# Ten of 24 state products of a scan chunk on VectorE instead of eight, and the engines' orders laid out anew

## The reference

```
delta = softplus(w_dt @ dts + b_dt)                # per batch, direction k, channel d, position t
h[t] = exp(delta[t] * A[d,n]) * h[t-1] + delta[t] * u[t] * B[n,t]
y[t] = sum over n of h[t] * C[n,t]  +  D * u[t]    # 16 states n, 192 channels d, 4096 positions t
```

## Time and profile before

| | us |
|---|---|
| median of 3 runs | 11698.7 (11697.71 to 11724.16) |
| the profiled execution | 11687.62 |
| its span | 11685.8 |
| VectorE busy | 10036.1 (86%) |
| GpSimd busy | 8772.1 (75%) |
| ScalarE busy | 8437.5 (72%) |
| TensorE busy | 9207.4 (79%) |

### The profile page before, as it was taken

One profiled execution on the slowest core, in us unless ns is written; L12 is line 12 of the kernel. 1 busy time (PEld: TensorE's weight loads), 2 busy tenths in 40 slices (PEclk: granted clock), 3 DMA queues, 4 the chain that ended last, 5 costly groups with the idle time before them and its releaser, 6 DMA issues. The chain is left out here.

```text
span 11685.8 us, 144402 instructions
## 1 busy us (share of the span) xinstructions
PE 9207.4 (79%) x34584; PEld 3443.5 (29%) x34584; DVE 10036.1 (86%) x6335; ACT 8437.5 (72%) x13829; POOL 8772.1 (75%) x4468
## 2 busy tenths in 40 slices
PE   8877777777777777777777777777777777588888
PEld 2322222222222222222222222222222222233333
DVE  7759999999899989999999899999999999866565
ACT  6767777777777777777777777777777777455555
POOL 0019999899899989999999899999999999521210
PEclk9988888888888888888888888888888888799999
DMA  3347777787777777777777777777777777643441
GB/s 103 122 127 185 183 187 184 178 187 186 183 180 185 187 183 181 186 187 183 184 185 188 179 183 185 185 182 181 185 186 184 187 186 182 149 112 94 100 108 49
DMA packets 577596, 1948.45 MB, mean 167 GB/s; under 512 B 106614, under 2 KB 111638, under 8 KB 562198
## 3 DMA queue, kind: packets, MB, share of 16 engines
q1 hardware_dynamic: 573714, 1938.65, 69.8%
q10 hardware_dynamic: 3076, 0.97, 0.1%
HBM read 1532.38 MB, written 406.85 MB: 166 GB/s over the span
## 5 line engine op out<-in xcount | busy, mean ns | idle before, releaser
L1108 POOL TENSOR_TENSOR dBu<-rep,shared 128x1024 f32<-128x1024 f32 x2304 | 4552.5, 1998 | 886.2 <-DMA rep<-dd_dram 833.5
L1116 POOL TENSOR_TENSOR h<-h,shared 128x1024 f32<-128x1024 f32 x2048 | 4020.7, 1972 | 728.6 <-DVE h L1068 728.0
L893 ACT ACTIVATE pd<-rep,a_now 128x1024 f32<-128x1024 f32 x2304 | 2556.1, 1109 | 362.7 <-DVE h L1068 200.9
L821 PE MATMUL py<-h,fold 128*32 128x512 f32 x8192 | 2447.8, 701 | 214.9 <-ACT y L968 214.9
L1068 DVE TENSOR_TENSOR_SCAN h<-pd,carry,dBu 128x1024 f32<-128x1024 f32 x960 | 2242.4, 2344 | 409.7 <-ACT pd L893 280.0
L1068 DVE TENSOR_TENSOR_SCAN pd<-pd,carry,dBu 128x1024 f32<-128x1024 f32 x768 | 1795.8, 2338 | 0.1
L821 PE MATMUL py<-shared,fold 128*32 128x512 f32 x3072 | 1479.6, 880 | 221.8 <-ACT y L968 173.3
L934 ACT ACTIVATE shared<-shared,turned_b 128x192 f32<-128x192 f32 x4096 | 1553.2, 442 | 15.5 <-ACT shared L921 5.4
L799 PE MATMUL pd<-eye,shared 128*128 128x128 f32 x6144 | 1006.9, 316 | 619.3 <-DVE h L1068 466.9
L1068 DVE TENSOR_TENSOR_SCAN h<-h,carry,pd 128x1024 f32<-128x1024 f32 x576 | 1308.8, 2326 | 43.2 <-PE pd L799 32.3
L799 PEld LDWEIGHTS pd<-eye,shared 128*128 128x128 f32 x6144 | 792.8, 159 | 1083.4 <-DVE h L1068 478.0
(11 more groups left out here) (174 smaller groups left out, 14120.2 us busy)
## 6 DMA issues: line engine op xcount, KB each, us to landing
rep<-dd_dram SPq DMA_DIRECT2D x1024, 768.0 KB, 13.0
shared<-bc_dram SPq DMA_DIRECT2D x3584, 128.0 KB, 4.6
u<-u_dram SPq DMA_DIRECT2D x128, 768.0 KB, 6.8
dd_dram<-LG SPq DMA_DIRECT2D x256, 384.0 KB, 4.0
dd_dram<-RL SPq DMA_DIRECT2D x256, 384.0 KB, 5.1
y_dram<-y SPq DMA_DIRECT2D x256, 384.0 KB, 8.1
shared<-y_dram SPq DMA_DIRECT2D x63, 1536.0 KB, 15.7
u_dram<-shared SPq DMA_DIRECT2D x32, 1536.0 KB, 7.5
```

Source lines behind the costliest of these rows:

```text
L821: last = mm(py[32 * g:32 * g + 32, t2(t)], fold[:, :], weighted(3 * j + g, k)[:, t2(t)], start=(j % 4 == 0), stop=(j % 4 == 3), skip_group ...
L893: go(dst, rep[:, half, 0, g, :], ACT.Exp, scale=a_now[:, column(i)]).then_inc(S.exped, 1)
L1108: nc.gpsimd.tensor_tensor(dBu[:, ring(c, p), :], rep[:, half, 1, g, :], BB[:, r, :], ALU.mult).then_inc(S.dbu, 1)
L1116: nc.gpsimd.tensor_tensor(turned(weighted(i, k), k), turned(kept(i, k), k), turned(CC[:, r, :], k), ALU.mult).then_inc(S.hc_pool, 1)
```

## The change

- `DVE_TILES` gains tiles 7 and 16. VectorE multiplies ten tiles of a chunk by C (eight so far), GpSimd fourteen (sixteen so far). `PLACES` goes from 8 to 7 and the product slots `PRODUCTS` from 4 to 5.
- TensorE's order: the first fold comes behind `add_up` of the next chunk's first half; `skip` comes behind the third fold; the fifth fold comes behind `add_up` of the second half.
- ScalarE's order: the copy of y's second half moves from step 2 to step 4, of the first half from 14 to 17; both copies of x_dbl and B now in step 23; `STEPS`, `SCALE` and `SCALE_NEXT` are shifted by a step or two.
- GpSimd's order: the two products fall out, and drives and products are interleaved anew.

```diff
--- before.py
+++ after.py
@@ -383,7 +383,7 @@
         psum = lambda name, shape: ctx.enter_context(nc.psum_tensor(name, shape, F32))
         S = a.sems
         BK = B * K
-        PLACES, PRODUCTS = 8, 4
+        PLACES, PRODUCTS = 7, 5
 
         a_neg, a_now = sb("a_neg", [128, K, NS]), sb("a_now", [128, NS])
         fold, eye128 = sb("fold", [128, 32]), sb("eye128", [128, 128])
@@ -408,7 +408,7 @@
         turned_b = sb("turned_b", [128, 2, TB, J])
         dBu = sb("dBu", [128, 4, T])
         h = sb("h", [128, PLACES, T + 4])
-        hC_last = sb("hC", [128, T])
+        hC_own = sb("hC", [128, PRODUCTS - 3, T])
         carry = sb("carry", [128, NS])
         y = sb("y", [HALF, T])
         pd = psum("pd", [128, 2, T])
@@ -427,7 +427,7 @@
 
         TRIPLES = ((0, 0), (0, 1), (0, 2), (0, 3), (1, 3), (1, 0), (1, 1), (1, 2))
         DRIVEN, TURNED, SCALED = 18, 6, 4 * TB
-        DVE_TILES = (0, 3, 4, 6, 15, 18, 19, 21)
+        DVE_TILES = (0, 3, 4, 6, 7, 15, 16, 18, 19, 21)
 
         def where(i):
             half, r = TRIPLES[i // 3]
@@ -459,7 +459,7 @@
             if is_kept(i):
                 return h[:, KEPT.index(i) % PLACES, 2:T + 2] if k < 2 else h[:, KEPT.index(i) % PLACES, 3:T + 3]
             slot = DVE_TILES.index(i) % PRODUCTS
-            return hC[:, slot, :] if slot < 3 else hC_last[:, :]
+            return hC[:, slot, :] if slot < 3 else hC_own[:, slot - 3, :]
 
         def state(i, k):
 
@@ -836,9 +836,9 @@
 
             def body(bk, k, c, left):
                 n, s = bk * NC + c, c % 2
-                reduce_states(n, k, 0)
                 if left:
                     add_up(n + 1, 0)
+                reduce_states(n, k, 0)
                 turn_back(bk, c, 9)
                 turn_back(bk, c, 10)
                 reduce_states(n, k, 1)
@@ -850,12 +850,12 @@
                 if left:
                     make_step(n + 1, 1)
                 turn_back(bk, c, 14)
+                reduce_states(n, k, 2)
                 skip(n, s, 0)
-                reduce_states(n, k, 2)
                 reduce_states(n, k, 3)
-                reduce_states(n, k, 4)
                 if left:
                     add_up(n + 1, 1)
+                reduce_states(n, k, 4)
                 skip(n, s, 1)
                 if left:
                     turn_du(n + 1, 1)
@@ -985,17 +985,16 @@
 
             STEPS = {1: [(absolute, 0)],
                      2: [(exp_abs, 0), (relu, 0), (one_plus, 0)],
-                     4: [(log, 0)],
-                     8: [(copy_delta, 0)],
+                     5: [(log, 0)],
+                     10: [(copy_delta, 0)],
                      11: [(copy_du, 0)],
-                     12: [(absolute, 1), (exp_abs, 1)],
-                     13: [(relu, 1)],
-                     14: [(one_plus, 1)],
-                     16: [(log, 1)],
+                     13: [(absolute, 1)],
+                     14: [(exp_abs, 1), (relu, 1), (one_plus, 1)],
+                     15: [(log, 1)],
                      18: [(copy_delta, 1)],
                      20: [(copy_du, 1)]}
-            SCALE = {0: 3, 2: 2, 3: 3, 4: 2, 5: 6, 6: 2, 7: 1}
-            SCALE_NEXT = {20: 5, 21: 3, 22: 2, 23: 3}
+            SCALE = {0: 3, 1: 2, 3: 2, 4: 4, 5: 2, 6: 6}
+            SCALE_NEXT = {20: 3, 21: 2, 22: 4, 23: 4}
 
             def run(bk, k, c, left, first, span):
                 n, s = bk * NC + c, c % 2
@@ -1010,14 +1009,14 @@
                         if c == NC - 1 and i + 2 == NS:
                             pick_a(bk + 1, (k + 1) % K)
                         expo(*((bk, k, c + 1) if c < NC - 1 else (bk + 1, (k + 1) % K, 0)), i + 2 - NS)
-                    if i == 2 and not first:
+                    if i == 4 and not first:
                         copy_y(n - 1, 1)
-                    if i == 14:
+                    if i == 17:
                         copy_y(n, 0)
                     if left:
                         for step, half in STEPS.get(i, ()):
                             step(n + 1, half)
-                        if left >= 2 and i == 22:
+                        if left >= 2 and i == 23:
                             copy_x_dbl(n + 2)
                         if left >= 2 and i == 23:
                             copy_b(n + 2, s)
@@ -1122,19 +1121,18 @@
             def body(bk, k, c, left):
                 n = bk * NC + c
                 drive(n, c, 3)
+                weigh(n, k, 1)
                 drive(n, c, 4)
-                weigh(n, k, 1)
+                drive(n, c, 5)
                 weigh(n, k, 2)
-                drive(n, c, 5)
                 drive(n, c, 6)
                 drive(n, c, 7)
                 drive(n, c, 8)
                 weigh(n, k, 5)
                 drive(n, c, 9)
                 drive(n, c, 10)
-                weigh(n, k, 7)
+                weigh(n, k, 8)
                 drive(n, c, 11)
-                weigh(n, k, 8)
                 weigh(n, k, 9)
                 weigh(n, k, 10)
                 weigh(n, k, 11)
@@ -1143,18 +1141,17 @@
                 weigh(n, k, 14)
                 drive(n, c, 12)
                 drive(n, c, 13)
-                weigh(n, k, 16)
+                drive(n, c, 14)
                 weigh(n, k, 17)
-                drive(n, c, 14)
                 drive(n, c, 15)
                 drive(n, c, 16)
                 drive(n, c, 17)
                 weigh(n, k, 20)
                 if left:
                     drive(n, c, 18)
-                    drive(n, c, 19)
                 weigh(n, k, 22)
                 if left:
+                    drive(n, c, 19)
                     drive(n, c, 20)
                 weigh(n, k, 23)
             chunk_loop(pool, body)
```

## The result

| | before | after |
|---|---|---|
| median of 4 runs each, us | 11702.44 | 11594.29 (11592.5 to 11613.69) |
| profiled execution, its span | 11687.62, 11685.8 | 11613.69, 11611.7 |
| scan phase, us a chunk | 72.49 | 71.75 |

The ratio is 0.9908 with a 95% interval of 0.9891 to 0.9925: 108 us faster, where 216 were forecast. The time lies within the range, the gain is half of what I had worked out. (The execution profiled after stands 20 us above its median.)

What follows compares the result with a forecast made beforehand. VectorE was taken to bound the kernel. Work 69.00 plus holes of 0.85, 0.3 and 0.65 gave 70.8 us a chunk against 72.49, 216 us less: 11472 profiled, 11482 in the median's terms; range 11370 to 11650.

Steps and rivals of the forecast that it cites:

- The work: VectorE's busy time a chunk: 66.35 us plus 2.65 for the two added products, 69.00 in all.
- The small rest: Small VectorE holes that remain: 0.65 us a chunk, a quarter of the 2.6 left of today's idling.
- the 70.6: VectorE's work a chunk, in us, by the rule that the next operation waits for an empty pipe; the sum didn't use it.
- ScalarE's new order: ScalarE's pieces laid along VectorE's scans: exponentials 3 to 9 ready in time, with cover of 0.2 to 1.5 us.
- Tile 5's hole: VectorE's wait before tile 5's scan, from ScalarE's queue order: goes with the copy of y moved, 3.0 us a chunk.
- The hole before tile 2: VectorE before tile 2's scan: a new hole of 0.85 us, its exponential ready at 6.3, VectorE at 5.75.
- C's third row: Load for tile 6's product on VectorE: lands some 20.1 into the chunk, wait 0.3 us, between 0 and 1.8.
- Rival (b): C's third row lands at 22.4, tile 6's product 1.8 us late: 72.3 a chunk, 11675, no difference; chance 0.10.
- the paragraph on TensorE: add_up before the first fold: ends at 23.7, tile 9's transposes done at 27.1, wanted 27.55; no cost, cover 0.4 us.
- the 26.5: Sign of being wrong on TensorE: transposes of tile 9 starting later than 26.5 us into the chunk.
- (c): Rival at ScalarE's chunk border: late X delays tile 2; slower, 75.1 a chunk, 12038, if all idle time stays; chance 0.10.

Runs made afterwards that it cites:

- e5: The kernel before with the products of tiles 7 and 16 moved to VectorE and all orders as before: 12070.36 us, ratio 1.032.
- e12: e11 with ten small idle matmuls in TensorE's wait for log in add_up, first half: 11350.65 us, ratio 0.9716 against the kernel before.
- e3: The kernel after with ScalarE's four scalings of step 23 put between the copies of x_dbl and B: 11522.35 us, ratio 0.9854 against before.
- e1: The kernel after with ten small idle matmuls ahead of TensorE's wait for log in add_up, first half: 11536.93 us, ratio 0.9863 against before.
- e4: The kernel after's new orders with eight tiles on VectorE, eight places and four slots: 11586.97 us, ratio 0.9906 against before.
- e7: The kernel after with the first fold inside add_up and e3's scalings between the copies: 11506.09 us, ratio 0.9847 against before.
- e11: e9 with the first fold put back behind add_up: 11395.86 us, ratio 0.9755 against the kernel before.
- e9: e7 with first-half delta's copy, its product with u, its store (before B's load) and y's first-half copy all earlier: 11459.47 us, ratio 0.9795 against before.
- e10: e9's earlier chain before the loads, with eight tiles on VectorE and sixteen on GpSimd: 11237.05 us, ratio 0.9609 against the kernel before.

## Why the prediction was half right

Term by term, for a chunk:

| | forecast | measured |
|---|---|---|
| work | 69.00 | 68.35 busy |
| tile 2 | 0.85 | 0.74 |
| tile 6's product | 0.3 | 0.28 |
| tile 9 | 0 | 1.17 |
| tile 14 | 0 | 0.29 |
| all else | 0.65 | 0.92, of which 0.64 in gaps of under 0.15 us each |
| sum | 70.8 | 71.75 |

- *The work* was 0.65 too high: VectorE is busy 2.0 us a chunk more than before instead of 2.65 (in e5 2.36). The small rest was 0.27 too low: gaps of under 0.15 us alone make 0.64 (0.70 before). e12, with most holes closed, does a chunk in 69.72, start to start, below the 70.6 that the prediction worked out from the drain. The Trainium skill ("VectorE: DVE Perf Modes", The DRAIN you can't avoid) says in the same paragraph that a next operation that is not held starts earlier, which the prediction left out; the scans that start every 2.24 with 2.33 of length agree with that.
- *ScalarE's new order* came out as laid down: 1+e ends 14.06 into the chunk (by my layout 14.05), log at 21.8 (21.9), the copy of y at 18.45 (18.4). Tile 5's hole went and the copy of y no longer waits for TensorE.
- *The hole before tile 2* was 0.74 for 0.85; its cause is shown by e3.
- *Loads.* C's third row lands at 20.35 (20.1 forecast), the wait 0.28 (0.3). Rival (b)'s later landing did not come.
- *The step that failed* is the paragraph on TensorE: "No cost, cover 0.4." I let `add_up` end at 23.7 and the fold take 1.95, tile 9's transposes done at 27.1 and wanted at 27.55. In 49 chunks this came out: 23.9, and done at 27.55 for a scan that is ready at 28.0. In 63 `add_up` ends at 25.5 and the transposes are done at 29.9, 2 us late; they start at 28.8, beyond the 26.5 that was named as a sign of being wrong. I had used durations at the full clock behind a wait that the change itself makes: in the old order TensorE came to the log late and found it ready (idle 0.0 in the group above), in the new one it comes early and idles. The hole is 1.17 us a chunk, more than the 0.95 that the sum is short; the other terms, of both signs, give 0.22 back. e1 shows the cause, and also that removing it gives 57 us (e12: 45) and not 1.03 x 128 = 132, as tile 14, tile 6's product and tile 2 take up part of what is won. Tile 14's 0.29 goes with the clock too, by the 28 chunks of 28 above; no run fills that wait, so there the cause is argued. That the time lies in the range at all is luck: the range had room for small holes that went, and the two behind the slow clock, 1.46 together, filled it.
- *What the sum left out* is that the loads stand next behind VectorE: what makes the chunk shorter brings a product or X nearer to its load (e3, e4, e7). The prediction had both places, as rivals (b) and (c) at 0.10 each. In after neither decides (X ends at 1.15 on average, wanted at 1.55); in the variants with less work or fewer holes they are the limit.
- Open: what decides in which chunks the clock falls (the third chunk of a direction keeps it in 21 cases of 28 in after, the others in 28 of 84, but in e11 the third in 10 of 28); which of e9's four moves freed the loads; and e10 with the ten idle matmuls wasn't tried.

## What to carry to other kernels

Where a new order puts a wait of some 2 us into TensorE's queue, price what follows at both clock levels, and see if the wait can be put where nothing urgent follows, or filled. Moving work into it can move the idle time to a dearer place (e9 against e11). When an edit takes a hole away, look for the transfer that the shorter loop runs into: here it took part of e3's and e7's gain, until the chain in front of the loads was moved up. When a load is put ahead, look at every load that stays behind, also those that come only once in four chunks. And test the two halves of a change apart: ten tiles looked free beside orders that were held up by loads, and cost 222 us when they weren't.

## What was not expected of the hardware

- Waits of 1.67 to 2.52 us on TensorE brought the granted clock to 0.50 to 0.56 in 63 chunks, and waits of 2.10 to 2.53 left it at 1.0 in 35 (after); ten matmuls of 128 columns in that wait kept it at 1.0 in every chunk (e1).
- Some 17 us later in the chunk, behind a wait of 1.3 us, tile 14's transposes ran below 0.75 of the clock in 28 of 112 chunks (after) and in 46 once the first wait was filled (e1), and each time VectorE waited before tile 14.
- A load of u behind eight loads of rows of B and C took 13 us from issue to landing, with the DMA engines' share at 0.96 to 1.09 in that time (e4).
